# Products of the identity in six waits of TensorE, before the main loop and behind it

## What is computed

```python
# block 1, three gated residual steps, modulated from cond
h = ln(x)*(1+sc)+sh;  x = x + g_msa * (softmax(q k / 4) v over shifted windows of 128 tokens, 16 heads) @ w_so
h = ln(x)*(1+sc)+sh;  x = x + g_mca * (softmax over the 16 largest of 77 context scores, per head, times v) @ w_co
h = ln(x)*(1+sc)+sh;  x = x + g_mlp * (silu(a) * b) @ w_m2
# block 2
nx = layernorm(x); evidence = softmax(nx Wq (ctx Wk)^T) (ctx Wv); combined = [nx, evidence, anchor]
routed = sum over 3 experts of router_prob * (silu(combined @ e_w1) @ e_w2)
x = x + sigmoid(silu(combined @ gate_w1) @ gate_w2) * (routed @ out_w + out_b)
```

## Time and profile before

| what | value |
|---|---|
| median of 3 runs | 1528.04 us (1523.42 to 1529.38) |
| the profiled execution's own time | 1530.62 us |
| its span | 1528.8 us |
| TensorE busy, matmul records | 1456.4 us, 95% of the span |
| VectorE, ScalarE, GpSimd busy | 1025.6, 836.5, 240.1 us |
| mean granted clock of TensorE | 0.968 of full speed |

### The profile page before, as it was taken

How to read it: one execution, slowest core, us unless ns; L and a number is a source line. 1 busy time by engine, 2 the same in 40 slices (tenths; PEclk the granted TensorE clock), 3 DMA queues, 4 the chain that set the end, 5 groups by cost and what they waited for, 6 DMA issues and landing times.

```text
span 1528.8 us, 32900 instructions
## 1 busy us (share of the span) xinstructions
PE 1456.4 (95%) x9793; PEld 1215.0 (79%) x9793; DVE 1025.6 (67%) x4678; ACT 836.5 (55%) x2546; POOL 240.1 (16%) x413
## 2 busy tenths in 40 slices
PE   5888699999999999999999999999999999999987
PEld 2656578888888888888888788888888888887876
DVE  4446685868768585867768585867768585857532
ACT  1415337574756537574756637484756637574423
POOL 2001210112123110111123110111123110111100
PEclk8866899999999999999999999999999999999999
DMA  8201000000000000000000000000000000000000
GB/s 298 78 28 49 2 1 2 18 2 22 8 15 29 17 1 2 18 2 22 8 15 29 17 2 2 18 2 22 8 15 29 15 1 2 8 2 8 1 8 8
DMA packets 25140, 31.70 MB, mean 21 GB/s; under 512 B 3051, under 2 KB 21627, under 8 KB 24443
## 3 DMA queue, kind: packets, MB, share of 16 engines
q1 hardware_dynamic: 24959, 29.52, 6.1%
HBM read 25.32 MB, written 4.19 MB: 19 GB/s over the span
## 4 chain that ended last, share of the span: by engine, by line
PE 73%; DVE 19%; issue 5%; ACT 1%; DVEq 1%; DMA 0%; POOL 0%; SPq 0%; POOLq 0%; ACTq 0%
PE bank L882 11%; PE bank L811 10%; PE bank L857 9%; PE bank L683 6%; DVE knocked L1978 5%; PE bank L864 5%; PE bank L821 5%; PE bank L668 4%; PE bank L742 4%; PE bank L730 4%; DVE M L1971 2%; PE bank L722 2%; DVE M L1966 2%; PE bank L676 2%; PE bank L639 2%
## 5 line engine op out<-in xcount | busy, mean ns | idle before, releaser
L811 PE MATMUL bank<-hB,Wm 128*128 128x256 f32 x1024 | 244.2, 385 | 3.7 <-issue 2.5
L811 PEld LDWEIGHTS bank<-hB,Wm 128*128 128x128 f32 x1024 | 191.9, 191 | 35.8 <-issue 11.9
L857 PE MATMUL bank<-nxT,W1nx 128*128 128x256 f32 x896 | 213.2, 384 | 0.0
L1249 ACT ACTIVATE prob<-bank,rmax 128x128 f32<-128x128 f32 x512 | 180.0, 435 | 32.9 <-DVE rmax L1928 32.9
L1256 ACT ACTIVATE probT<-bank 128x512 f32<-128x512 f32 (+1 forms) x256 | 141.4, 610 | 97.3 <-PE bank L795 76.0
L857 PEld LDWEIGHTS bank<-nxT,W1nx 128*128 128x128 f32 x896 | 167.2, 192 | 23.1 <-issue 2.8
L882 PE MATMUL bank<-W2p,gT 128*128 128x256 f32 x768 | 182.8, 381 | 0.0
L882 PEld LDWEIGHTS bank<-W2p,gT 128*128 128x128 f32 x768 | 144.0, 192 | 20.6
L1555 POOL TENSOR_TENSOR scores_or_ada<-scores_or_ada,M 128x308 f32<-128x308 f32 x128 | 94.8, 741 | 401.4 <-DVE knocked L1978 401.4
L1285 ACT ACTIVATE tbs<-bank,b1half 128x256 f32<-128x256 f32 x128 | 60.6, 473 | 150.9 <-PE bank L811 115.5
L1297 ACT ACTIVATE tbs<-bank,betaH 128x256 f32<-128x256 f32 x224 | 94.9, 484 | 85.7 <-PE bank L864 85.4
(11 more groups left out here) (231 smaller groups left out, 2530.4 us busy)
## 6 DMA issues: line engine op xcount, KB each, us to landing
Wm_g<-in_L_xcond_w_m_dram SPq DMA_DIRECT2D x4, 1024.0 KB, 5.2
W1ev<-in_L_xcond_e_w_dram SPq DMA_DIRECT2D x6, 512.0 KB, 7.1
x<-in_x_dram SPq DMA_DIRECT2D x16, 128.0 KB, 2.1
x<-in_x_dram SPq DMA_DIRECT2D x32, 64.0 KB, 2.6
Wm<-in_L_xcond_w_m_dram SPq DMA_DIRECT2D x1, 2048.0 KB, 12.7
out_dram<-acc SPq DMA_DIRECT2D x16, 128.0 KB, 1.8
out_dram<-acc SPq DMA_DIRECT2D x32, 64.0 KB, 2.0
W1nx<-in_L_xcond_e_w_dram SPq DMA_DIRECT2D x3, 512.0 KB, 13.5
```

The costliest lines, as they stand in the source:

```text
L811: m = pe.matmul(bank_of(name)[:, half * UT:(half + 1) * UT], Wm1[:, k, c:c + P], hB[:, k, :], start=(k == 0), stop=(k == CB - 1))
L857: pe.matmul(bank_of(name)[:, n * UT:(n + 1) * UT], W1nx[:, k, c0 + n * P:c0 + (n + 1) * P], nxT[:, k, :], start=(n == 0 and k == 0), stop= ...
L1249: m = act.activation(prob[:, s, i, :], psum[s][:, i * P:(i + 1) * P], ACT.Exp, bias=rmax[:, t, s * HPS + i:s * HPS + i + 1], accum_out=rsu ...
```

## The change

A function `idle_products(n)` is added. It multiplies the 128x128 identity by itself n times into bank 6 of PSUM, in ordinary float32 matmuls, signals nobody and is read by nobody. It is called at six places of TensorE's program: four in `second()` with 12, 8, 16 and 18 products, one in `last_cross` with 13 and one in `last_experts` with 16, 83 in all. Three waits are added ahead of them so that bank 6 is free: for the reading of the folding job M0, and twice for h10's turn in that bank. Nothing else moves; the loop is as it was.

```diff
@@ -889,6 +889,11 @@
                 bias_first("g2", "g2")
                 pe.wait_ge(gated, u * len(FIRST_ORDER) + len(FIRST_ORDER))
                 token_major("g2", gs, Wg2, CB)
+
+            def idle_products(n):
+
+                for i in range(n):
+                    pe.matmul(psum[6][:, (i % 4) * P:(i % 4 + 1) * P], ident[:, :], ident[:, :], start=True, stop=True)
 
             def first():
 
@@ -947,6 +952,8 @@
                     a_turn_probs(0, s, 1)
                 a_values(0, 1)
                 a_scores(1, range(SLOTS), 1)
+                pe.wait_ge(fold_read, FOLD_JOBS.index("M0") + 1)
+                idle_products(12)
                 for s in range(SLOTS):
                     a_turn_probs(1, s, 1)
                 a_turn_inverses("r1", "pv", 1)
@@ -954,6 +961,7 @@
                 a_project("pv", oT, "so", Wso_g, 1)
                 for s in range(SLOTS):
                     a_turn_picked(0, s, 0)
+                idle_products(8)
                 a_turn_query(1)
                 a_query(1)
                 a_cross_values(0, 0)
@@ -961,8 +969,10 @@
                     a_turn_picked(1, s, 0)
                 a_turn_inverses("r2", "xv", 0)
                 a_cross_values(1, 0)
+                idle_products(16)
                 pe.wait_ge(gatedC, 2)
                 a_project("xv", oT2, "co", Wco_g, 0)
+                idle_products(18)
                 turn("ln3", xnB, 0, normed[2], TILES)
                 pe.wait_ge(wb_loaded, 16 * (len(wb_loads) + len(evidence_loads)))
                 pe.wait_ge(prepared_b, 1)
@@ -1104,6 +1114,8 @@
                 b_down(7, b)
                 a_turn_picked(0, 0, c)
                 a_turn_picked(0, 1, c)
+                wait_free(pe, "h10", b)
+                idle_products(13)
                 b_turn_normed(b)
                 a_turn_picked(0, 2, c)
                 a_turn_picked(0, 3, c)
```

## The result

The changed kernel takes 1519.01 us (median of 20 runs, 1516.57 to 1526.63), the kernel before 1527.82 (median of 20, 1523.31 to 1529.78). The ratio of the runs is 0.9957, with a 95% interval of 0.9945 to 0.9970: 4.6 to 8.4 us less, 6.6 in the middle. The profiled execution took 1518.37 us, its span 1516.6. The ratio is taken over all the runs and is not the quotient of the two medians, which is 0.9942 here: with runs in groups the median jumps from one group to the other, so the gain is judged by the ratio.

What follows compares the result with a forecast made beforehand. TensorE bounds the loop at full clock; outside it, half-clock stretches after waits cost time. Terms 1.9 + 2.4 + 0 + 0 + 0.7 + 2.8 = 7.8 us; forecast 1521.0, between 1520.2 and 1522.8; range 1516 to 1526.

Steps and rivals of the forecast that it cites:

- the case that it rested on: Clock holds at the last four of six groups; median gains 4 to 9 us, 1519 to 1524; chance 0.72.
- Price of a product: One 128-column product takes 0.21 to 0.25 us at full clock, taken as 0.215; about 0.43 at half clock.
- Place 3: 16 products in second() before projection co: bias matmul and projection at full clock give back 1.9 us.
- Place 4: 18 products in second(): 0.3 us at ln3's transposes, 2.1 at the loop's first hidden layer; together 2.4.
- Places 1 and 2: 12 and 8 products in second(): both taken as 0; the first has an upper bound of 0.95 us.
- The rule on transposes: Behind the first 12 products: transposes don't count as busy like matmuls, so the clock falls again, without the 0.95 us.
- Place 5: 13 products in last_cross: 0.7 us given back, the rest becoming a wait for ScalarE's copy before the values.
- Place 6: 16 products in last_experts: transposes 0.15, prototype scores 0.96, experts' first layer 1.7; together 2.8 us.
- The last stretch: Half-clock stretch 1498.86 to 1502.22, no products ahead: stays or moves, 0, with 1.5 us as upper bound.
- The sum: Over all six groups: 1.9 + 2.4 + 0 + 0 + 0.7 + 2.8 = 7.8 us given back.
- The third: Products don't hold the clock, or VectorE and ScalarE take most: gain 0 to 3 us, 1525 to 1528; chance 0.13.
- The fourth: Products run at half clock and overrun their waits by 16.7 us in all, making 1544.7; chance 0.03.

Runs made afterwards that it cites:

- tail-only kernel: Kernel 1: changed kernel without the four groups ahead of the loop and the M0 wait, keeping 13 and 16 products behind it; 1521.37 us, ratio 0.9958 to the kernel before.
- thin products: Kernel 10: kernel 8 with each product moving 4 columns instead of 128; 1532.26 us, ratio 1.0037 to the kernel before.
- doubled kernel: Kernel 4: changed kernel with every group twice as long (24, 16, 32, 36, 26, 32 products); 1532.17 us, ratio 1.0037 to the kernel before.
- kernel 5: Changed kernel without the first group of 12 products and the wait for M0; 1519.08 us, ratio 0.9955 to the kernel before.
- kernel 7: Kernel 6 plus five products in the wait ahead of the loop's first hidden layer; 1520.84 us, ratio 0.9950 to the kernel before.
- kernel 8: Changed kernel with only the groups of 16 and 18 products in second(), M0 wait ahead of them; 1525.69 us, ratio 0.9997 to the kernel before.
- kernel 9: Kernel 8 with the group of 8 products in second() put back; 1522.94 us, ratio 0.9978 to the kernel before.
- kernel 11: Kernel 7 plus 6, 6, 5, 6, 5 and 4 products in six earlier waits; 1510.98 us, ratio 0.9894 to the kernel before.
- kernel 12: Kernel 11 plus two products behind every fourth of the 28 matmuls of the anchor's folding; 1514.95 us, ratio 0.9920 to the kernel before.
- kernels 2: Changed kernel with only the four groups ahead of the loop (12, 8, 16, 18) and the M0 wait; 1525.29 us, ratio 0.9994 to the kernel before.
- kernel 3: Changed kernel with twice as many transposes of the identity in place of the products, all six groups; 1523.18 us, ratio 0.9977 to the kernel before.
- kernel 6: Changed kernel plus three products behind each of the four transpose groups that follow the first 12 products; 1517.41 us, ratio 0.9942 to the kernel before.

## Why the prediction was right, and where it was not

The measured 1519.01 lies in the range, 2.0 below the forecast, and the case that it rested on is the one that holds: the products keep the clock and the matmuls behind them run at full speed. The tail-only kernel shows it where it pays, the thin products show, at place 3, that it takes the moved columns and not the weight loads alone. Below the median of before the forecast put 7.0 us; the medians give 8.8 and the ratio 6.6. By its steps:

**Price of a product.** The doubled kernel gives it free of any wait: (166.48 - 159.23) / 32 = 0.227 us, inside the bounds of 0.21 and 0.25 and above the 0.215 that I took. It cost nothing: the distances from the engine's previous work to the next are 3.80, 4.13, 3.11 and 3.71 at places 3 to 6 against waits of 3.80, 4.13, 3.11 and 3.70. Place 1 overran by 0.4 and lost nothing by it. At 0.227 the groups of places 3 to 6 fit with 0.05 to 0.17 us to spare, and doubling them shows what an overrun costs.

**Place 3.** 1.9 predicted, 7.80 - 5.91 = 1.9 measured.

**Place 4.** 0.3 + 2.1 = 2.4 predicted; 0.25 + 0.35 in the changed profile, 0.25 + 2.0 in kernels 5, 7, 8, 9, 11 and 12. Here the step failed in part: I let the products carry the clock over ScalarE's wait of 1.26 us, which is in the earlier trace rows and has none. The clock fell in the first 0.05 to 0.4 us of the hidden layer in the changed kernel and in kernels 2, 3 and 6, and not in 5, 8 and 9, with the same program in that wait (7, 11 and 12 have five products in it). It was a gamble written down as a certainty.

**Places 1 and 2.** I took 0 for place 1, with 0.95 as the bound, and read the earlier trace rows as a clock that can survive transposes. The profile shows 0.81 won (a 9.92). But kernels 2 and 3 show 2.1 us lost in b by the same products, and kernel 5 no loss without them. My bound should have gone below zero: the price of a fall that comes later, over the projection so. The rule on transposes that I weighed there, that of the Trainium skill's page "TensorE: Matmul & The Clock Gate" ("Part 4: PE-mode transpose"), doesn't explain the fall: full rows of transposes held the clock in kernel 3, and in kernel 6 the short groups did with products in the 0.74 us between them.

**Place 5.** 0.7 predicted, with a new wait for ScalarE's copy in front of the values of about 1 us: 0.69 and 0.81. **Place 6.** 2.8 predicted, 2.7 measured.

**The last stretch.** I took 0 and kept 1.5 as the bound: 1.5 was given back (i 36.95 for 38.42). Nothing was changed in that stretch, and the profiles fall in two groups: 36.9 us in the changed kernel and in kernels 1, 3, 4, 6, 10 and 12, 38.4 to 38.6 in the kernel before and in 2, 5, 7, 8, 9 and 11. With place 6's products it was the lower one in six of nine, without them in one of five (the thin kernel), which is too few to call it an effect of theirs.

**The sum.** 7.8 was made of 1.9 + 2.4 + 0.7 + 2.8; the same terms are 1.9 + 0.6 + 0.7 + 2.7 = 5.9 in the profile, and 8.2 with place 1's 0.8 and the last stretch's 1.5. The measured centre is 6.6. That the total came so close is partly luck: place 4 gave 1.8 less than its term, and two terms that I had put at 0 gave 2.3. That the profile of before was an unlucky execution I had read from its distance to the median; what was unlucky is now seen: its start, 136.74, where ten of the twelve profiles with an unaltered program up to there have 130.8 to 132.9. That start is 5 us longer, as much as the two groups of the kernel before lie apart; that the one makes the other is likely and not shown, since only one execution of a kernel has a profile.

**The rivals.** The third, that the products don't hold the clock, is out. The fourth, slower, has its mechanism shown in the doubled kernel by overrun and in the thin one by half clock; with the change's counts it occurred at none of places 3 to 6 in the profiles. My reason against it misread one row: the wait of place 4 began at 170.45 in the kernel before, while the clock was at 0.50 until 171.08. At place 4 the clock was up only because place 3 kept it. What I had nowhere was a fall in front of the loop that moves, and the price of the loop's position.

**Which groups carry it.** The two behind the loop alone give 0.9958. Places 2, 3 and 4 alone give 0.9978, places 1 to 4 0.9994, so place 1 looks like a cost there; but the two intervals share 0.9978 to 0.9994, and kernel 5 against the changed one shows none, so it is not shown. Front and tail together, with or without place 1, give 0.9957 and 0.9955, and not the 0.9936 that 0.9958 and 0.9978 would multiply to; that lies just outside both intervals, by 0.0003 to 0.0009, but the factors have intervals of their own. Whether front and tail add up stays open.

## What to carry to other kernels

Cut two profiles at the same events before you compare them, and compare them ahead of the edit too: here 4.9 of 12.2 us lay there. If TensorE's granted clock drops in a dependency chain, fill the waits with matmuls that move many columns (128 held it here, 4 did not), a little shorter than the wait, and fill the small waits of a stretch with the large one: a lone filled wait can just move the fall onto a matmul on the path, while kernel 11, with the small waits filled as well, gained 15.5 us of median. Look for half-clock stretches ahead of the place that was edited; the largest were there.

## What the runs showed of the hardware

- A stretch in which TensorE is busy throughout can lose its clock: 32 records with 128 columns of weights and 4 moved columns went from 1.00 to 0.50 after 1.7 us of the group (kernel 10). The anchor's folding, 56 records with 4 moved columns and no wait, lost it 0.9 to 3.5 us after its start in all 14 profiles (in kernel 12 with products between them).
- A float32 record with 128 columns of weights starts every 0.112 us at a clock of 1.00 and every 0.213 us at 0.50 in kernel 10, where it moves 4 columns; in kernel 8, where it moves 128, it is 0.112 at 1.00 as well.
- Float32 transposes of 128x128 in a row held the clock at 1.00 as float32 products did (kernel 3: projection of co at 1.89, c 5.90, h 6.29).
- The loop's return costs TensorE a wait of 1.1 to 1.7 us, and 2.4 once (the doubled kernel's second return). In the two kernels with 34 extra products ahead of the loop, 8 and 10, a second wait of 1.2 to 1.5 us appears behind the body's first group, whether the products move 128 columns or 4: the units with the return take 86.6 to 87.4 us. With 0, 42, 54, 66, 71, 103 or 117 products they take 85.2 to 85.8. What in the layout makes the second wait is open.
